# One transfer per image row for turned K and turned Q, centred output weights, and a new issue order on every engine

## The reference, cut to what matters

```python
def step(carry, inp):
    W1c, b1c = carry
    xq, xk, xv, et = inp
    Z1 = xk @ W1c + b1c
    grad = _ln_l2_bwd(Z1, xv - xk, g, bb)
    Attn1 = jnp.tril(xq @ xk.swapaxes(-1, -2))
    b1_bar = b1c - jnp.tril(et) @ grad
    Z1_bar = xq @ W1c - et * Attn1 @ grad + b1_bar
    last_eta = et[..., -1, :, None]
    W1n = W1c - (last_eta * xk).swapaxes(-1, -2) @ grad
    b1n = b1c - (last_eta * grad).sum(-2, keepdims=True)
    return ((W1n, b1n), xq + _ln(Z1_bar, g, bb, EPS_IN))
...
return _ln(out, post_w, post_b, EPS_IN) @ o_w.T
```

## Time and profile before

| | us |
|---|---|
| median of 3 runs | 2009.25 (2008.76 to 2012.17) |
| profiled execution, span from first to last instruction | 2010.2 |
| PE busy | 1569.5 (78%) |
| DVE busy | 1582.3 (79%) |
| POOL busy | 1317.2 (66%) |
| ACT busy | 977.5 (49%) |

### The profile page before, as it was taken

How to read it: one execution, slowest core, us unless ns; L and a number is a source line. 1 busy time by engine, 2 the same in 40 slices (tenths; PEclk the granted TensorE clock), 3 DMA queues, 4 the chain that set the end, 5 groups by cost and what they waited for, 6 DMA issues and landing times.

```text
span 2010.2 us, 82699 instructions
## 1 busy us (share of the span) xinstructions
PE 1569.5 (78%) x33518; PEld 1214.9 (60%) x33518; DVE 1582.3 (79%) x3818; ACT 977.5 (49%) x2358; POOL 1317.2 (66%) x1479
## 2 busy tenths in 40 slices
PE   1886978914678887888788888878887888888886
PEld 1443544502567676677676766766776766767664
DVE  6989998706687877788878878887888788788774
ACT  2223545443455555555555545555555555555452
POOL 1244535465677777777767777777777777677763
PEclk9998989965666667666656666666666666666655
DMA  6058697962555655556656556666565566566553
GB/s 235 1 30 44 98 98 68 77 159 45 65 70 66 76 71 68 73 67 77 74 65 77 70 69 74 72 71 73 67 77 73 67 77 73 65 76 73 69 68 44
DMA packets 1656796, 148.89 MB, mean 74 GB/s; under 512 B 1636448, under 2 KB 1650016, under 8 KB 1656416
## 3 DMA queue, kind: packets, MB, share of 16 engines
q1 hardware_dynamic: 1396912, 117.90, 49.9%
q10 hardware_dynamic: 259504, 25.70, 10.1%
HBM read 40.71 MB, written 38.54 MB: 39 GB/s over the span
## 4 chain that ended last, share of the span: by engine, by line
SPq 54%; PE 17%; DVE 12%; DMA 7%; issue 6%; POOL 3%; ACT 2%; POOLq 0%; DVEq 0%; ACTq 0%
SPq L486 25%; SPq L519 13%; SPq L479 12%; DMA late<-work 3%; PE p_m L1678 3%; PE p_x L1693 3%; DMA xs_scratch<-work 2%; SPq L438 2%; PE p_j L1557 2%; DVE work L1007 2%; SPq L440 1%; DVE work L1033 1%; PE p_y L1736 1%; PE p_y L1693 1%; PE p_out L1752 1%
## 5 line engine op out<-in xcount | busy, mean ns | idle before, releaser
L1648 PE MATMUL p_kt<-fold,kqk 128*128 128x16 f16 x6272 | 199.4, 174 | 166.9 <-DMA kqk<-work 162.8
L1648 PEld LDWEIGHTS p_kt<-fold,kqk 128*128 128x128 f16 x6272 | 190.6, 104 | 197.9 <-issue 161.3
L808 ACT ACTIVATE work<-p_kt 128x512 f16<-128x512 f32 x196 | 146.9, 750 | 317.8 <-PE p_kt L1648 317.8
L1557 PE MATMUL p_j<-work 128*128 128x392 f16 x864 | 158.5, 345 | 22.2 <-DVE work L1131 20.7
L578 POOL TENSOR_TENSOR work<-work,row 128x256 f32<-128x256 f32 x98 | 96.9, 988 | 113.2 <-DVE work L1437 113.2
L1316 DVE TENSOR_TENSOR work<-work 128x256 f16<-128x256 f32 x196 | 155.2, 842 | 15.4 <-ACT work L795 15.4
L1621 PE MATMUL p_j<-wa,work 128*128 128x512 f16 x196 | 119.4, 609 | 58.4 <-DMA work<-xs_scratch_tail 30.0
L590 POOL TENSOR_TENSOR w<-wst,w 128x256 f16<-128x256 f32 x98 | 75.5, 770 | 127.8 <-ACT w L855 127.8
L1693 PEld LDWEIGHTS p_x<-w,late 128*128 128x128 f16 x4704 | 149.5, 106 | 12.0
L634 POOL TENSOR_TENSOR work<-work,rope_s 128x256 f32<-128x256 f32 x196 | 141.0, 740 | 20.0 <-DVE work L1283 20.0
L645 POOL TENSOR_TENSOR work<-work 128x512 f32<-128x512 f32 x98 | 130.8, 1335 | 30.4 <-DVE work L1307 30.1
(11 more groups left out here) (171 smaller groups left out, 4474.3 us busy)
## 6 DMA issues: line engine op xcount, KB each, us to landing
late<-work SPq DMA_DIRECT2D x1176, 32.0 KB, 2.7
kqk<-work SPq DMA_DIRECT2D x392, 64.0 KB, 4.2
out_y<-work ACTq DMA_DIRECT2D x49, 256.0 KB, 6.4
x_scratch<-late SPq DMA_DIRECT2D x24, 392.0 KB, 11.7
xs_scratch<-work SPq DMA_DIRECT2D x24, 392.0 KB, 6.7
work<-x_scratch ACTq DMA_DIRECT2D x49, 192.0 KB, 3.4
work<-xs_scratch SPq DMA_DIRECT2D x48, 192.0 KB, 3.4
late<-in_x SPq DMA_DIRECT2D x8, 784.0 KB, 9.0
```

What stands on the lines that cost most here:

```text
L808: return act.activation(kqt16[:, o, g:g + GP, :, :, :].rearrange("p g h t a -> p g a (h t)"), p_kt[:, :].rearrange("p (g a n) -> p g a n", ...
L1557: mm = pe.matmul(p_conv[b % 2][h][:, 0:HALF].rearrange("o (i j) -> o i j", j=W), convw16[:, w, t, :], pad[:, b % 2, a, r:r + ROWS, c:c + W ...
L1648: mm = pe.matmul(p_kt[:, at:at + CS], part_of(g + k, h, a), fold16[:, :], start=True, stop=True)
```

## The change

It joins `kt_spread` and `qt_spread` into `turned_spread`: 8 transfers of 64 KB per chunk in place of 16 of 32 KB, the same bytes in the same runs of 64 bytes. The joined transfers wait for the copies of both K and Q, and all three users on PE wait for the one semaphore. The output weights are centred once, in the convolution stage, by one more matmul and one more DVE subtraction; `post_shift` goes, and `post_norm` only scales. The turn lists of all five engines are written anew; SP's and PE's are shown in full, of ACT's the part around the copies. DVE's loses the two `post_shift` and is otherwise a new order of the same names, POOL's too.

```diff
-            def kt_spread(c):
+            def turned_spread(c):
                 sp.wait_ge(kt_copy_done.sem, kt_copy_done.count(2 * c + 1))
+                sp.wait_ge(qt_copy_done.sem, qt_copy_done.count(2 * c + 1))
                 if c < 2:
                     sp.wait_ge(s_kt_zero[c], 1)
                 else:
                     sp.wait_ge(z_done.sem, z_done.count(2 * c - 3))
                     sp.wait_ge(k_dot_q_done.sem, k_dot_q_done.count(c - 2))
-                turned_spread(c, 1, kt_landed.sem(c))
-
-            @guard_chunk
-            def qt_spread(c):
...
                     sp.wait_ge(o_done.sem, o_done.count(2 * c - 3))
-                turned_spread(c, 0, qt_landed.sem(c))
+                part = kqt16[:, :, :, :, :, :].rearrange("p o g h t a -> p (o g h) (t a)")
+                whole = ktqt[c % 2][:, :, :, :, :, :, :].rearrange("p o g h b t a -> p (o g h) b (t a)")
+                for b in range(GB):
+                    at = slice(b * CS, (b + 1) * CS)
+                    sp.dma_start(whole[at, :, b, :], part[at]).then_inc(turned_landed.sem(c), 16)
...
             def turn(k):
+                kq_spread(k - 3)
                 m_spread(k - 4)
-                kt_spread(k - 3)
-                qt_spread(k - 3)
-                kq_spread(k - 2)
                 xs_next(k)
+                turned_spread(k - 3)
...
             def post_norm(s):
-                act.wait_ge(post_shift_done.sem, post_shift_done.count(s))
+                act.wait_ge(post_inverse_done.sem, post_inverse_done.count(s))
...
-                    last = act.activation(on[:, k * C:(k + 1) * C], oo[:, k * C:(k + 1) * C], ACT.Identity, bias=ostd[:, 2, k:k + 1],
-                                          scale=ostd[:, 1, k:k + 1])
+                    last = act.activation(on[:, k * C:(k + 1) * C], oo[:, k * C:(k + 1) * C], ACT.Copy, scale=ostd[:, 1, k:k + 1])
...
+                folded(dve.tensor_tensor(wo_p[:, :], wo_p[:, :], p_x[1][:, SC:SC + C], ALU.subtract))
...
+                pe.matmul(p_x[1][:, SC:SC + C], mean_m, wo_p[:, :], start=True, stop=True).then_inc(s_fold, 1)
...
             def k_dot_q(c):
-                pe.wait_ge(kt_landed.sem(c), kt_landed.count(c))
-                pe.wait_ge(qt_copy_done.sem, qt_copy_done.count(2 * c + 1))
+                pe.wait_ge(turned_landed.sem(c), turned_landed.count(c))
```

More of the change, by code:

```diff
@@ L281, in program @@
         kq_landed = landed("kq_blocks", 2, GB)
-        kt_landed = landed("kt_blocks", 2, GB)
-        qt_landed = landed("qt_blocks", 2, GB)
+        turned_landed = landed("turned_blocks", 2, GB)
         m_landed = landed("m_blocks", 1, GB)
@@ L668, in turn @@
             def turn(k):
+                g_hat(2 * k - 5)
+                g_dot(2 * k - 5)
+                rope_sin(2 * k - 1)
+                o_scaled(2 * k - 7)
+                g_both(2 * k - 5)
+                rope_sum(2 * k - 1)
+                k_scaled(2 * k - 1)
+                o_sum_q(2 * k - 7)
+                w_low(2 * k - 6)
+                target(2 * k - 1)
+                q_out(2 * k - 1)
+                b_low(2 * k - 6)
                 rope_sin(2 * k)
@@ L671, in turn @@
                 o_sum_q(2 * k - 6)
+                rope_sum(2 * k)
+                b_low(2 * k - 5)
+                w_low(2 * k - 5)
+                g_scaled(2 * k - 4)
+                g_hat(2 * k - 4)
+                g_dot(2 * k - 4)
+                k_scaled(2 * k)
+                target(2 * k)
+                q_out(2 * k)
                 g_both(2 * k - 4)
-                rope_sum(2 * k)
-                k_scaled(2 * k)
                 g_scaled(2 * k - 3)
[L676 to L696, removed]
+            for k in range(NCH + 4):
                 turn(k)
@@ L1526, in turn @@
                 z_hat(2 * k - 3)
-                z_rate(2 * k - 3)
-                post_inverse(2 * k - 6)
-                g_low(2 * k - 4)
-                o_sum(2 * k - 5)
-                b_step(2 * k - 4)
-                post_shift(2 * k - 6)
+                norm(2 * k + 1)
+                g_low(2 * k - 4)
+                rope_cos(2 * k + 1)
+                o_hat(2 * k - 5)
+                g_means(2 * k - 3)
+                g_centre(2 * k - 3)
+                g_along(2 * k - 3)
+                b_step(2 * k - 4)
+                z_rate(2 * k - 3)
+                w_step(2 * k - 4)
+                g_rated(2 * k - 3)
+                rate_scaled(k)
+                final(2 * k - 7)
+                g_low(2 * k - 3)
+                qk_low(2 * k + 1)
+                post_stats(2 * k - 5)
                 if k == 1:
                     zero_late()
-            for k in range(NCH + 5):
+            for k in range(NCH + 4):
                 turn(k)
@@ L1754, in turn @@
             def turn(k):
+                project(2 * k - 1)
                 z_state(2 * k - 6)
-                out_project(2 * k - 10)
                 k_dot_q(k - 3)
+                outputs(2 * k - 7)
+                fold_k(2 * k - 4)
                 z_state(2 * k - 5)
-                project(2 * k - 1)
-                outputs(2 * k - 7)
+                fold_k(2 * k - 3)
+                rate_project(k - 1)
                 post_turn(2 * k - 9)
-                rate_project(k - 1)
-                fold_k(2 * k - 4)
+                fold_q(2 * k - 4)
                 out_project(2 * k - 9)
-                fold_k(2 * k - 3)
+                fold_q(2 * k - 3)
                 grad(2 * k - 6)
-                fold_q(2 * k - 4)
                 project(2 * k)
+                outputs(2 * k - 6)
                 post_turn(2 * k - 8)
-                fold_q(2 * k - 3)
-                outputs(2 * k - 6)
                 grad(2 * k - 5)
+                out_project(2 * k - 8)
             for k in range(NCH + 5):
```

116 lines of the change are left out of this document (36 added, 80 removed).

## The result

The changed kernel takes 1992.15 us (median of four runs, 1989.56 to 1996.18) against 2009.26 of the kernel before in the same session: a ratio of 0.9903, with a 95% interval of 0.9885 to 0.9921. It is faster by 17 us, less than 1% and about four times what such a measurement can tell from no change, where 126 were forecast. The profiled execution took 1991.81 us, its span is 1989.7.

The account below looks back on a forecast made before the run. SP's issuing was taken as the bound, 30.73 us per chunk. The new loop, 11.8 + 8.5 + 7.6 + 0.2 = 28.1 us, saves 126 us over 48 periods, giving 1883 us; range 1780 to 1945.

Parts of the forecast that it names:

- The loop of the prediction: SP's kq, PE's folds with the copies, SP's turned block, then the next kq: a closed loop of 28.1 us per chunk.
- The copies' 8.5: From the first fold on PE to the end of the last copy: 8.5 us, against 9.45 before the change.
- the turned block's 7.6: SP's block of 8 joined 64 KB issues: 7.6 us, within 6.8 to 9.25, replacing 14.37 us of 16 issues.
- The pause of SP: SP would wait about 4 us between xs and turned, until ACT's copies release the turned block.
- kq, first issue to first fold: From SP's first kq issue to PE's first fold: 11.8 us, lower end 9.0, upper end 12.3.
- a second way round: kq(c+2) also waits for the second grad of chunk c on PE; this way was put at the loop's length.
- The first and last chunks left as they are: The time before 495 us and after 1970 us was taken as unchanged by the edit.
- The hand-overs: The two hand-overs around the turned block in the loop: about 0.2 us together.
- m behind kq: On SP, m(c) now stands behind kq(c+1), landing some 5 us after it; claimed to cost nothing, as PE has 10.7 us of earlier work.
- Rival 1: kq too is issued in a short block and PE becomes the bound: period 26.1 us, 1787 us; chance 0.20.
- Rival 2: SP waits too long for the Q copies ahead of turned, next kq queued behind: loop 31.2, 2032 us; chance 0.08.
- Rival 3: A joined 64 KB issue takes twice a 32 KB one: block 14.4 us, loop 34.9, 2209 us; chance 0.03.

Follow-up runs that it names:

- 1937.22: Changed kernel storing only 4 of 32 images of each output chunk, so ACT's 256 KB store becomes 32 KB: 1937.22 us (one run).
- the last experiment: Changed kernel with ACT's store moved, three ACT list edits (spare tile 256 bytes), earlier DVE zeroing, load ahead of first Q copy: 1898.42 us, ratio 0.9455.
- 2154.78: Changed kernel with three edits of ACT's list, including a spare square root whose 216-byte tile moves later tiles by 32 bytes: 2154.78 us (one run).
- 2011.33: Changed kernel with the three edits of ACT's list, the spare tile made 256 bytes so later tiles are aligned again: 2011.33 us (one run).
- 2112.24: Changed kernel with ACT's store and load moved plus three edits of ACT's list, spare tile of 216 bytes: 2112.24 us, ratio 1.0538.
- 1912.15: Changed kernel with ACT's store and load moved plus three edits of ACT's list, spare tile of 256 bytes: 1912.15 us, ratio 0.9512.

## Why the prediction was wrong in size

**What held.** SP's queue was the bound before, and the join with the new lists ended that. The loop of the prediction (kq, folds and copies, turned, kq) exists, and where its blocks are long it is what sets the period: with the join taken out (32.67) and at the shifted address (33.37) kq starts 0.18 us behind turned in every chunk. The copies' 8.5 was 8.23, the turned block's 7.6 was 7.96. The pause of SP is there, about 4 us as forecast, but in two parts: 2.29 us ahead of m and 1.45 ahead of turned in the timeline above. post_shift was worth 5 us where I had nothing.

**The step that failed** is the first term, "kq, first issue to first fold" at 11.8. It measured 13.36, 1.56 us more per chunk or 75 us in 48 periods. I wrote that ACT's transfers "keep their number and now come nearer to the kq block, which is why I keep kq at 11.8 and not lower": I saw the change and priced it at nothing, by carrying over a row in which the store lay 16.7 us after kq's first issue. The upper end of 12.3 came from the same rows, and so was too low as well. What nearness costs could not be read in the kernel before, but the lists hint at it: ACT's new list has the store far ahead of the copies, and kq is now issued first in the turn. The runs show the price: without most of the store, 55 us; with the store behind kq and the load away from turned, 94 us (1992.15 to 1898.42; ACT's order and the earlier zeroing, which that kernel has too, gave nothing by themselves). How much of the step from 55 to 94 us is transfers, and how much is that ACT's list was freed of two issues at the old places, was not separated.

**A path that was left out.** The prediction let kq start 0.1 us behind turned, and looked for a second way round only over grad on PE. The way over z_state and DVE's list to qk_low was not added up; I wrote that what the order of the lists can add is inside the 8.5 and the range. In the kernel after this way releases kq in 30 of 39 chunks, and once kq is short (1937.22 and 1898.42) the engines end last, at 29.05 and 28.1 us. The first of the two is the test: kq landed 11.2 us after its first issue, sooner than a first term of 11.8 needs, and the period was still 29.05. So the first term alone, had it been right, would not have given the forecast's time.

**The smaller terms.** The hand-overs were 0.76 and not 0.2, since kq waits for qk_low and grad as well: it starts 0.19 us after the one and 0.42 after the other on average, so the way round over grad, which I had put at the same length, is indeed close behind. "The first and last chunks left as they are" failed in both directions: 11.6 us more at the start, 5.9 less at the end. At the start the new DVE list fills the blocks with zeros ahead of the norm that project, and behind it z_state(0), waits for; moving the fill moved the delay and did not end it, so the start stays open. Together, against the forecast span of 1884.0: 48 x (30.18 - 28.1) + 11.6 - 5.9 = 105.5, and 1989.5 for the 1989.7 seen.

**The steps priced at nothing.** That m behind kq costs nothing holds, though not for the reason given: it waits 2.5 us per chunk for the outputs of the chunk before, in a pause in which SP would have waited for the copies anyway. z_state's wait was forecast at 0.4 us per chunk and is 12.2/48 = 0.25.

**The rivals.** Rival 1 (PE the bound) did not come: PE waits 3.7 us of each period. The granted clock did not rise with fewer waits but fell, 0.62 to 0.57. In the last experiment it is close to coming: PE is busy 84% of the span, the fold waits for kq 9 times instead of 36, and PE has the largest share of the chain, with DVE next. Which of these two would have to become faster was not tried. Rival 2's place exists (SP waits 55.3 us for copies) but not its size: its 31.2 needed folds and copies of 9.45 us, and they took 8.23. Rival 3 (a 64 KB issue takes twice a 32 KB one) is out: the blocks are 7.96 against 13.14 for the 16 issues at the same place. Beside that row, the sentence of the Trainium skill, DMA: Bandwidth & Descriptors, "Issuing engines are not separate DMA queues", on the small time of initiating a transfer does not fit this kernel. Its other sentence there, that transfers of all issuing engines end up on the same 16 DMA engines and interleave, fits what made the miss: a store issued by ACT lengthened the issues of SP. I had used the sentence against the change as a whole, and had not asked which transfers would now interleave with kq's.

**One part without the other.** "I give the order no price of its own" was the other error of method: the join without the order is 90 us slower than before. With the new lists the join pays (118 us), and they are also what laid the store on kq; both belonged in the sum.

## What to carry to other kernels

When a queue that issues transfers stops being the bound, draw every closed loop that can replace it and add its terms, those over the engines too. A sum of terms that follow each other equals the period by construction; look at who released the first instruction of each term to see whether that loop is the one. For each transfer in the loop list what the other queues issue in the same microseconds, because a block's duration depends on them. Then move the transfers that nobody waits for (a store, a load with a period to spare) to the stretch between the blocks. When an unrelated edit makes all transfers slower, compare the addresses of the tiles.

## What had not been expected of the hardware

**32 bytes of address.** The transfers place runs of 64 bytes. With their tiles moved by 32 bytes the kernel took 2142.71 instead of 1992.15 us, the same kernel otherwise; two more pairs differ in the same way alone: 2154.78 against 2011.33 and 2112.24 against 1912.15. The pages show it in the packets of SP's queue (packets, MB, share of the time of 16 engines), first the kernel after, then the shifted one:

```profile
q1 hardware_dynamic: 1390640, 117.87, 51.0%
...
q1 hardware_dynamic: 1390640, 117.87, 56.2%
```

The same packets with the same bytes took 0.562 x 2140.9 = 1203 us on each of the 16 engines in the mean, against 0.510 x 1989.7 = 1015, so 19% more. The other two pairs come to 19% as well (56.6% of 2152.7 against 51.0% of 2009.5, and 55.9% of 2103.2 against 51.8% of 1909.4). The Trainium skill, DMA: Bandwidth & Descriptors, "How a descriptor splits into AXI transactions", says that a transaction starts at an address that is a multiple of 256 bytes, so that a piece crossing such a border is split. By that, runs of 64 bytes at multiples of 64 never cross, and at 32 bytes beside them one in four does, which makes a quarter more transactions, as an estimate. The direction agrees with the 19%, and so, roughly, does the size. The blocks grow less evenly: turned 9.92 over 7.96 and kq 11.76 over 10.26 here, 9.13 over 8.30 and 9.08 over 7.61 in the last pair. That the splitting is the cause, and which of the moved tiles counts, no run here shows.

**One queue's issue time depends on another queue's transfers.** The first two 64 KB issues of a kq block took 1.37 and 1.85 us right behind a 256 KB store from another queue, and 0.76 and 0.82 with the store cut to 32 KB at the same place.

**The clock.** In the kernel after TensorE waits less and was granted less: 0.57 of full in the stretch against 0.62, a mix of 1.2 and 2.4 GHz in both. PE is busy about 1 us more per chunk with the same matmuls (26.5 against 25.5); how much of that lies on a loop was not measured.
